# Gate logits and second bias of a language-model tower from half-precision pieces, and the lookahead scores moved ahead of the value products

## The reference

```python
h = _L0_tok_ref(x, W, b)                                   # embedding + position
h = h + _L0_attn_ref(_layernorm(h), ...)                   # 8 heads, causal, no softmax
# second block, on _layernorm(h):
q, k = l2norm(q) * scale * qn_g, l2norm(k) * scale * kn_g  # 2 heads of 64
attn = softmax(where(causal, q @ k.T * dh ** -0.5, min))
y = (attn @ v) @ Wo
gate = softmax(y @ gate_W + gate_b)                        # 8 experts
hid = gelu(einsum('bnd,edf->bnef', y, W1) + b1)            # 8 x 512
eo = einsum('bnef,efd->bned', hid, W2) + b2
h = h + einsum('bned,bne->bnd', eo, gate)
```

## Time and profile before

| | |
|---|---|
| median of 3 runs | 854.6 us (852.33 to 855.84) |
| the profiled execution | 854.43 us, its span 852.6 us |
| PE, DVE, ACT, POOL busy | 785.5, 710.0, 479.0, 340.6 us |
| chain that ended last | PE 79%, DVE 8%, ACT 5% |
| mean granted clock of PE | 0.98 of full speed |

### The profile page before, as it was taken

The page is one execution under the profiler, slowest core; times in us unless marked ns, Lnnn a source line. Parts: engine busy times, 40 slices in busy tenths (PEclk is TensorE's granted clock), DMA queues, the critical chain, the costliest instruction groups (busy, mean ns, idle before and its releaser), DMA issues.

```text
span 852.6 us, 21002 instructions
## 1 busy us (share of the span) xinstructions
PE 785.5 (92%) x8208; PEld 557.8 (65%) x8208; DVE 710.0 (83%) x1585; ACT 479.0 (56%) x997; POOL 340.6 (40%) x386
## 2 busy tenths in 40 slices
PE   2799999999876788998999889999999999999997
PEld 1578778887644455655556557777777777777775
DVE  3548988888689776777677888999999999999997
ACT  2335555555345567777888756455555555555553
POOL 6638999877564547665667630000000000000000
PEclk9779999999999899999999999999999999999999
DMA  4100111000000000000000000000000000000000
GB/s 129 56 8 19 39 38 35 16 26 27 13 1 0 2 2 2 2 3 2 2 14 3 2 2 2 2 14 2 13 2 14 2 14 2 14 2 14 2 14 13
DMA packets 9666, 12.09 MB, mean 14 GB/s; under 512 B 1856, under 2 KB 6592, under 8 KB 9568
## 3 DMA queue, kind: packets, MB, share of 16 engines
q1 hardware_dynamic: 8544, 8.65, 3.5%
q0 software_dynamic: 1024, 2.10, 0.9%
HBM read 8.65 MB, written 2.10 MB: 13 GB/s over the span
## 4 chain that ended last, share of the span: by engine, by line
PE 79%; DVE 8%; ACT 5%; issue 4%; POOL 2%; DMA 1%; DVEq 0%; ACTq 0%
PE ps L988 77%; DVE mx L834 2%; DVE room L942 1%; DVE room L944 1%; ACT room L562 1%; ACT qk L492 1%; DVE mx L829 1%; DMA h_all<-emb_rows,idx 1%; PE ps L996 1%; DVE och L911 0%; PE ps L1016 0%; ACT qh L499 0%; ACT hxT L481 0%; ACT kh L501 0%; PE ps L1305 0%
## 5 line engine op out<-in xcount | busy, mean ns | idle before, releaser
L577 ACT ACTIVATE cst<-ps,col 128x512 f32<-128x512 f32 x256 | 175.9, 688 | 163.5 <-PE ps L988 162.7
L988 PEld LDWEIGHTS ps<-arena,sq 128*128 128x128 f16 x3072 | 192.0, 98 | 61.9 <-DVE sq L972 4.3
L988 PE MATMUL ps<-arena,sq 128*128 128x128 f16 x3072 | 213.2, 219 | 0.5 <-DVE sq L972 0.5
L988 PE MATMUL ps<-y,arena 128*128 128x512 f16 x768 | 208.6, 382 | 1.3 <-DVE och L911 1.3
L972 DVE TENSOR_TENSOR sq<-cst,sq 128x512 f16<-128x512 f32 x256 | 176.0, 688 | 4.4
L373 POOL TENSOR_TENSOR room<-room 128x512 f16<-128x512 f32 (+3 forms) x122 | 123.2, 1028 | 76.8 <-ACT room L562 76.2
L967 DVE CAST sq<-cst 128x512 f16<-128x512 f32 x256 | 109.1, 426 | 11.4 <-ACT cst L577 4.1
L834 DVE TENSOR_REDUCE mx<-ps 128x2 f32<-128x1024 f32 (+2 forms) x64 | 70.2, 1097 | 38.5 <-PE ps L988 38.2
L553 ACT ACTIVATE room<-ps 128x512 f32<-128x512 f32 (+3 forms) x160 | 76.7, 533 | 44.1 <-PE ps L988 42.6
L988 PEld LDWEIGHTS ps<-y,arena 128*128 128x128 f16 x768 | 64.9, 98 | 34.2 <-issue 3.7
L988 PEld LDWEIGHTS ps<-v,room 128*128 128x128 f16 x1632 | 58.2, 98 | 42.0 <-issue 21.5
(11 more groups left out here) (158 smaller groups left out, 1185.6 us busy)
## 6 DMA issues: line engine op xcount, KB each, us to landing
sq<-w_rows SPq DMA_DIRECT2D x16, 256.0 KB
out<-h_all SPq DMA_DIRECT2D x32, 64.0 KB, 1.6
cst<-consts SPq DMA_DIRECT2D x1, 896.0 KB
h_all<-emb_rows,idx POOLq DMA_INDIRECT x32, 4.9
cst<-consts SPq DMA_DIRECT2D x1, 398.0 KB, 3.5
c<-consts SPq DMA_DIRECT2D x1, 256.0 KB, 5.3
wqkv<-w_qkv SPq DMA_DIRECT2D x1, 192.0 KB
wsm<-w_sm SPq DMA_DIRECT2D x1, 192.0 KB, 5.5
```

The costliest lines, as they stand in the source:

```text
L577: a.activation(hid[:, f], ps[:, HBANK[f], :], ACT.Gelu_apprx_tanh, bias=col[:, K_B1 + k:K_B1 + k + 1], scale=1.0 / WS).then_inc(S["hid_rea ...
L988: return t_.matmul(o, l, r, start=start, stop=stop, skip_group_check=True)
```

## The change

The gate logits of an item are computed from `yhi`, `ylo` and two half-precision pieces of `64 * gate_W` (three products per 128 rows, 12 small matmuls in place of four 32-bit ones, now reading `ylo`); DVE divides by 64 when it adds the gate bias. The gates are split into two half-precision pieces by two more DVE instructions, laid beside each other as high, high, low (96 columns for 4 blocks, 8 experts, 3 pieces), transposed by one half-precision product with `-I`, and multiplied with `b2h`, in which `b2` stands as high, low, high: one half-precision matmul over 96 rows and 512 columns in place of four 32-bit ones. `wg16` is made by DVE in `step_b`, `b2h` by POOL between `step_b` and the attention. The offsets of the output chain are moved by a step for the logits and what follows; the transpose of the gates and the product with `b2` keep their places on PE. And where a step has one pair of pair scores, this pair now stands directly behind the scores, ahead of both value products (and ahead of `max_row`), where it stood between the two.

```diff
+            pool.wait_ge(S["load_s"], 80)
+            g.tensor_copy(b2h[:], b2s[:]).then_inc(S["b2_hi"], 1)
+            pool.wait_ge(S["b2_hi"], 1)
+            middle = slice(4 * E, 8 * E)
+            g.tensor_tensor(b2h[middle], b2s[middle], b2h[middle], ALU.subtract).then_inc(S["b2_ready"], 1)
+            pool.wait_ge(S["b2_ready"], 1)
...
-                    a.activation(gT[:], ps[0:4 * E, 5, 0:P], ACT.Copy, scale=WS).then_inc(S["gT_sb"], 1)
+                    a.activation(gT[:], ps[0:12 * E, 5, 0:P], ACT.Copy, scale=-1.0).then_inc(S["gT_sb"], 1)
...
+                if c == 8:
+                    dve.wait_ge(S["load_s"], 80)
+                    v.tensor_scalar(wg16[:, 0], wgate[:], WS, None, ALU.mult).then_inc(S["wg_hi"], 1)
+                if c == 9:
+                    dve.wait_ge(S["wg_hi"], 1)
+                    v.scalar_tensor_tensor(wg16[:, 1], wgate[:], WS, wg16[:, 0], ALU.mult, ALU.subtract
+                                           ).then_inc(S["wg_ready"], 1)
...
                     v.scalar_tensor_tensor(gs[:, m], gt[:, 1], 1.0 / WS, gl[:, 2].unsqueeze(2).to_broadcast([P, 4, E]),
-                                           ALU.mult, ALU.mult).then_inc(S["gate_ready"], 1)
+                                           ALU.mult, ALU.mult).then_inc(S["gh_link"], 1)
+                    dve.wait_ge(S["gh_link"], 2 * m + 1)
+                    v.tensor_scalar(g16[:, 0:2], gs[:, m].unsqueeze(1).to_broadcast([P, 2, 4, E]), WS, None, ALU.mult
+                                    ).then_inc(S["gh_link"], 1)
+                    dve.wait_ge(S["gh_link"], 2 * m + 2)
+                    v.scalar_tensor_tensor(g16[:, 2], gs[:, m], WS, g16[:, 0], ALU.mult, ALU.subtract
+                                           ).then_inc(S["gate_ready"], 1)
...
                 if j == 3:
                     pe.wait_ge(*bank5)
-                    pe.wait_ge(S["yhi_ready"], m + 1)
+                    pe.wait_ge(S["wg_ready"], 1)
+                    pe.wait_ge(S["ylo_ready"], m + 1)
                     for r in range(4):
-                        last = mm(ps[:, 5, r * E:(r + 1) * E], y32[:, r * P:(r + 1) * P], wgate[:])
+                        o, at = ps[:, 5, r * E:(r + 1) * E], m * CH + r * P
+                        mm(o, yhi[:, at:at + P], wg16[:, 0], stop=False)
+                        mm(o, yhi[:, at:at + P], wg16[:, 1], start=False, stop=False)
+                        last = mm(o, ylo[:, at:at + P], wg16[:, 0], start=False)
                     last.then_inc(S["lg_ps"], 1)
...
-                    t_.transpose(ps[0:4 * E, 5, 0:P], gs[:, m].rearrange("p r e -> p (r e)"), ident).then_inc(S["gT_ps"], 1)
+                    mm(ps[0:12 * E, 5, 0:P], g16[:].rearrange("p z r e -> p (z r e)"), minus16).then_inc(S["gT_ps"], 1)
...
-                    for r in range(4):
-                        last = mm(ps[:, 5, r * D:(r + 1) * D], gT[:], b2s[:, r * D:(r + 1) * D])
-                    last.then_inc(S["b2_ps"], 1)
+                    pe.wait_ge(S["b2_ready"], 1)
+                    mm(ps[:, 5, :], gT[:], b2h[:]).then_inc(S["b2_ps"], 1)
...
-                for part in pairs[:-1]:
+                for part in pairs[:1]:
                     pair_scores(*part)
...
-                if len(pairs) == 1:
-                    pair_scores(*pairs[0])
...
-PE_Y, ACT_Y, DVE_Y = [1, 2, 3, 7, 8], [1, 2, 4, 7], [3, 5, 9]
+PE_Y, ACT_Y, DVE_Y = [1, 2, 4, 7, 8], [1, 2, 5, 7], [4, 6, 9]
```

More of the change, by code:

```diff
@@ L62, in tower @@
         wgate = sb("wgate", [P, E])
-        b2s = sb("b2s", [4 * E, 4 * D])
+        b2s = sb("b2s", [12 * E, 4 * D])
+        b2h = sb("b2h", [12 * E, 4 * D], F16)
+        wg16 = sb("wg16", [P, 2, E], F16)
         mhalf = sb("mhalf", [P, 16])
@@ L159, in tower @@
         gl = sb("gl", [P, 3, 4])
-        gT = sb("gT", [4 * E, P])
+        g16 = sb("g16", [P, 3, 4, E], F16)
+        gT = sb("gT", [12 * E, P], F16)
         sqf = sq[:].rearrange("p b h j -> p (b h j)")
@@ L178, in tower @@
             lg_ps lg_link lg_ready eg_ready gate_ready gT_ps gT_sb b2_ps h2_ready hid_ps hid_ready hhi_ready
-            hlo_even hlo_odd l2_link x_sb v_link ao_link w2_done eo_used stored"""
+            hlo_even hlo_odd wg_hi wg_ready b2_hi b2_ready gh_link l2_link x_sb v_link ao_link w2_done eo_used stored"""
         S = {name: sem(name) for name in names.split()}
@@ L882, in out_part @@
                     dve.wait_ge(S["lg_ps"], m + 1)
-                    v.tensor_tensor(gt[:, 0], lg, row[:, R_GB:R_GB + E].unsqueeze(1).to_broadcast([P, 4, E]), ALU.add
-                                    ).then_inc(S["lg_link"], 1)
+                    v.scalar_tensor_tensor(gt[:, 0], lg, 1.0 / WS, row[:, R_GB:R_GB + E].unsqueeze(1)
+                                           .to_broadcast([P, 4, E]), ALU.mult, ALU.add).then_inc(S["lg_link"], 1)
                     dve.wait_ge(S["lg_link"], 4 * m + 1)
@@ L1552 @@
         b2[r, :, r] = a["L0_ffn_b2"]
-    b2 = b2.reshape(4 * E, 4 * D)
+    b2 = np.tile(b2.reshape(4 * E, 4 * D), (3, 1))
     arrays = {
```

## The result

The changed kernel took 860.2 us (median of 4 runs, 858.5 to 861.4) against 854.0 us for the kernel before (852.3 to 855.8) on the same chip: a ratio of 1.0067, with a 95% interval from 1.0047 to 1.0088. It is slower, by 6 us; the forecast was 849.4 us.

What follows compares the result with a forecast made beforehand. PE was taken to set the pace in most steps. Terms -5.6 - 4.0 + 4.3 - 3.7 + 2.5 + 1.5 gave -5.0 us against 854.4, so 849.4 us, own range 845 to 852, wider range 842 to 857.

Steps and rivals of the forecast that it cites:

- the new wait for `ylo`: PE at the end of step `YAT+4` waits for POOL's `low_y`: 7.7 us in sum, net +4.3, bounds +1 and +9.
- given back: Part of the `ylo` waits not lost: 1.6 us at item 0, 1.4 at item 6, half a microsecond at item 5.
- second rival: It nets to nothing: the wait for `ylo` at its bound, +9, against the rest, 854 us; chance 0.27.
- slow rival: End of step `YAT+4`: waits for `ylo` cost 13.5 us net or more; 862.6 us at 17.5 us; chance 0.06.
- the second bias: One half-precision matmul replaces eight records on PE: 0.87 us saved for each of 8 items, -5.6 us taken as real.
- The transpose of the gates: On PE, it stays one instruction and was counted at nothing.
- DVE's two instructions: Two more DVE instructions per item, 0.4 to 0.5 us with their waits, partly waited for: +1.5 us.
- this holding as a rival: DVE held by POOL: 16 new instructions held by 0.8 us, half on the path, +6.4 us, 855.8 us; chance 0.05.
- logits -4.0 us: On PE, twelve half-precision matmuls at 0.47 us replace 0.96 us of logits: 0.5 us per item, -4.0 us.
- Pair order and its waits: Single-pair steps on PE: one array change fewer in 46 steps, -3.7 us; pairs waiting for DVE's maxima, +2.5 us.
- its case: The forecast itself: 849.4 us, range 845 to 852, chance 0.48; 0.7 of it counted as faster.
- the first rival: All of it pays: `ylo` wait taken from standing waits, pairs never stand; -15 us, 839.3 us; chance 0.14.

Runs made afterwards that it cites:

- the filling: Logits-only kernel plus idle matmuls, products thrown away, ahead of PE's waits on `ylo` for items 0, 4, 5 and 6: 1.0006 of the kernel before.
- the pieces made out of PSUM: Kernel before with only the second bias changed, gates transposed thrice in 32 bits, ScalarE rounding, DVE making low rows from PSUM: 0.9952 of before.
- the kernel with `low_y` early: Changed kernel with POOL's low half of y moved ahead of its low halves of the probabilities: 850.9 us, 0.9934 of the kernel before.

## Why the prediction was wrong

The step that failed is the price of the new wait for `ylo`: "Net +4.3 us". As a wait it was sized well (7.7 us in sum forecast; 9.4 us in the changed kernel, 7.8 with the logits alone). Net of what was given back the forecast had 4.3 (its own terms give 4.2), and with the clock out of it the runs have 4.2; at 3.3 us of uncertainty so close a match is in part luck. Left out was what an idle PE brings behind it: the granted clock. The forecast says nothing of the clock at all, and the filling shows it at 4.9 us for this wait. The whole term is 9.1 us, at the forecast's own bound of +9, with which its second rival has 854 us. It does not reach the 13.5 us from which the forecast's slow rival decides; the rest comes from the second bias, whose terms were off by more.

That is the second failure: "The transpose of the gates stays one instruction and is counted at nothing", and DVE's two instructions at +1.5 us. The transpose now needs what DVE makes through two instructions that take 0.9 us longer each when POOL is at work beside them: 8.4 us for the sixteen of the changed kernel, where sixteen of 0.19 us are 3.0. What PE asks of DVE next, gates or maxima, is late by it. The forecast named this holding as a rival, at 0.05, and priced it without the clock behind PE's waits. Second bias and DVE together were forecast at -4.1 us and measured at +3.1 us (0.9956 to 0.9992) beside the half-precision logits, +3.5 us with a step more between pieces and transpose, and -1.8 us alone, where the same sixteen took 5.7 us. The forecast's size was met only with the pieces made out of PSUM, 4.1 us saved. The product's row came near its price too, 0.31 us to the next start for 0.22.

The Trainium skill ("SBUF — State Buffer", section "Who interferes with whom") says that DVE and GpSimd share a pair of ports to SBUF. A `tensor_scalar` can contend for it by its two-port mode, and an instruction with two inputs in SBUF contends with a GpSimd instruction that reads SBUF; one with at most one input in SBUF, outside these modes, does not. The traces agree: the two new instructions went to 1056 and 1145 ns, the multiplication with two inputs in SBUF to 1181 ns, and the one that reads PSUM and one input in SBUF took 289 ns all eight times. The forecast cited the section and used it for a rival alone; it should have asked of each new instruction where its operands lie.

The other terms: logits -4.0 us, measured -3.8 with the wait gone. Pair order and its waits -1.2 us, measured -1.8 alone and -5.0 in the kernel with both other edits; a step with one pair takes 2.03 us now (420.49 to 422.52), under the 2.14 forecast. The forecast counted 0.1 us for one change between scores and values; the 24 value products in one run also take 0.84 us (421.68 to 422.52) where two runs of twelve took 0.47 each. For 46 steps that is 9.7 us in place of 4.6, against which PE's waits on maxima grew by 5.4 us in the kernel with this edit alone and by 6.8 us beside the other two edits, where the forecast had 2.5. Why the order is worth more there isn't settled: the interval of that difference is some 3 us wide on each side, and a part of it may be clock again, since its mean over 12 runs is 0.974 with the old order and 0.978 with the new. The preparations on POOL take 0.61 and 1.15 us ahead of its first low halves; no run takes them or the larger load out by themselves, so that they cost nothing is not shown. In the forecast's chances, 0.7 of its case and the first rival are 0.48, where it writes 0.49.

Summed as measured, -3.8 + 4.2 + 4.9 for the logits, +3.1 for the second bias and -5.0 for the pair order give +3.4 us; the changed kernel showed +5.7 in four runs and +2.0 in twelve. With the interval of either that is the same number. It is less of a proof than it looks: -3.8, +3.1 and -5.0 give the kernel with `low_y` early by the way they were measured, and only the 9.1 us come from another kernel, the one with the logits alone. In the changed kernel itself moving `low_y` gave 7.6 us. So the loss is accounted for within the intervals; the split between its terms is good to some 3.5 us each.

## What to carry to other kernels

- When a wait is put on TensorE, price the wait and what its clock does behind it. Here waits of 7.8 us in sum, up to 2.6 us each, cost 9.1 us, over half of it by the clock behind them. The cure was to bring the producer forward in its own queue; throwaway matmuls in the gap gave back half of it.
- When an instruction is late, moving its consumer is worth little if the same engine is waited for next by another name. Look at what holds the engine: here, instructions on operands in SBUF that went from 0.19 to over 1 us while GpSimd was at work.
- One profiled execution shows where the clock fell, not how often it does. Use the mean granted clock of many runs.

## What the runs showed of the hardware

The mean granted clock of an execution goes with the idle stretches of TensorE, and the time with the clock. Within the runs of one kernel, the ones at a lower clock are mostly the longer ones. The kernel before, in the group with the single edits, took 860.2 to 863.9 us in the three runs at a mean clock of 0.970, and 853.1 us in the one at 0.984. Between kernels, mean over 12 runs: 0.9697 with the logits edit alone, 0.9772 with its waits filled; 0.9715 for the changed kernel, 0.9792 with its waits filled; 0.976 to 0.978 for the kernel before.

The lower clock came in short stretches in these traces, mostly behind PE's idle stretches of 1.5 to 2.6 us, now and then behind shorter ones (the second bias alone, 344 and 443 us, behind 0.5 and 0.8 us). Such an idle stretch is no sure sign: from 300 to 500 us the changed kernel's profile has nine of 1.5 us and more, of which five were followed by half clock and four were not, 1.98 us at item 4 among them, and the kernel before has three, none of them followed by it. Equal ones were followed by it in one execution and not in another. From a mean clock of 0.9697 to one of 0.9772 it would be 6.5 us of 864 if PE set the pace all through; 4.9 us were measured, which is no less by its interval.

The filling matmuls were chosen about as long as the waits or shorter; no run shows what longer ones cost. At item 6 nine of them, 1.98 us, left 0.53 us of a 2.6 us wait.
